# One tile of the selective scan filled by TensorE and ScalarE instead of through DRAM

## The reference

```
x = x + 0.5 * ffn(layernorm(x))      # fp4 quantised, 256 -> 704 -> 256
x = x + mixer(layernorm(x))          # selective scan, below
x = x + 0.5 * ffn(layernorm(x))
```

```
xz = h @ in_proj_w;  u, z = split(xz);  u = silu(causal_conv(u))
dt, B, C = split(u @ x_proj_w);  delta = softplus(dt @ dt_proj_w + b)
h_t[d, n] = exp(delta_t[d] * A[d, n]) * h_{t-1}[d, n] + delta_t[d] * u_t[d] * B_t[n]
y_t[d] = sum_n h_t[d, n] * C_t[n] + u_t[d] * D[d]
out = (y * silu(z)) @ out_proj_w
```

## Time and profile before

| | us |
|---|---|
| device time, median of 3 runs | 3021.85 (3017.2 to 3024.54) |
| device time of the profiled execution | 3027.0 |
| its span, first to last instruction | 3025.2 |
| PE busy | 2607.9 (86%) |
| DVE busy | 2569.9 (85%) |
| POOL busy | 2276.9 (75%) |
| ACT busy | 1756.1 (58%) |
| mean granted TensorE clock | 0.90 of full speed |

### The profile page before, as it was taken

The page is one execution under the profiler, slowest core; times in us unless marked ns, Lnnn a source line. Parts: engine busy times, 40 slices in busy tenths (PEclk is TensorE's granted clock), DMA queues, the critical chain, the costliest instruction groups (busy, mean ns, idle before and its releaser), DMA issues. The chain is left out here.

```text
span 3025.2 us, 31486 instructions
## 1 busy us (share of the span) xinstructions
PE 2607.9 (86%) x10147; PEld 1368.9 (45%) x10147; DVE 2569.9 (85%) x2435; ACT 1756.1 (58%) x2337; POOL 2276.9 (75%) x1348
## 2 busy tenths in 40 slices
PE   4999999967878878878878879879877669999998
PEld 2666657633424424424425425425422126666665
DVE  7888875539999999999999999999999967777775
ACT  3554444447766766766767766767765434444442
POOL 4766664249989989989989899899899855655652
PEclk9999999978979979979979979979967679999999
DMA  3111111038898898888988988988988940011000
GB/s 112 32 53 42 53 49 35 24 101 213 196 220 204 204 220 198 209 213 200 213 215 200 218 212 198 214 207 208 217 197 203 233 97 28 29 35 35 28 29 21
DMA packets 183588, 424.67 MB, mean 140 GB/s; under 512 B 23952, under 2 KB 91472, under 8 KB 183184
## 3 DMA queue, kind: packets, MB, share of 16 engines
q1 hardware_dynamic: 164544, 402.19, 54.1%
q10 hardware_dynamic: 18896, 20.65, 2.4%
HBM read 341.88 MB, written 55.71 MB: 131 GB/s over the span
## 5 line engine op out<-in xcount | busy, mean ns | idle before, releaser
L1475 POOL TENSOR_TENSOR mix_scan<-mix_scan,mix_bc 128x1024 f32<-128x1024 f32 x512 | 1199.3, 2358 | 180.3 <-DVE mix_scan L1572 180.0
L1572 DVE TENSOR_TENSOR_SCAN mix_scan<-mix_decay,ps_all 128x1024 f32<-128x1024 f32 x512 | 1166.5, 2284 | 71.4 <-ACT ps_all L1516 24.4
L885 PE MATMUL ps_all<-ffn_w_gate_up,ffn_xT 128*128 128x512 f32 (+1 forms) x1536 | 654.0, 562 | 13.7 <-DVE ffn_h L612 9.4
L1525 ACT ACTIVATE mix_decay<-mix_decay,mix_a_neg 128x1024 f32<-128x1024 f32 x512 | 575.0, 1142 | 105.1 <-DMA mix_decay<-delta_rows 103.6
L1626 PE MATMUL ps_all<-mix_stack,mix_sel 96*128 96x512 bf16 x896 | 317.6, 442 | 322.5 <-DVE mix_scan L1572 309.2
L1582 DVE TENSOR_TENSOR ps_all<-ps_all,mix_bc 128x1024 f32<-128x1024 f32 x448 | 541.0, 1208 | 20.6 <-PE ps_all L1626 20.5
L885 PEld LDWEIGHTS ps_all<-ffn_w_gate_up,ffn_xT 128*128 128x128 f32 x1536 | 278.6, 192 | 245.9 <-issue 201.1
L758 POOL TENSOR_TENSOR ffn_h_scaled<-ffn_h,ffn_h_recip 128x1408 f32<-128x1408 f32 x64 | 168.6, 2635 | 243.6 <-ACT ffn_h_recip L853 243.6
L1608 PE MATMUL ps_all<-mix_scan,mix_red 128*32 128x512 f32 x2048 | 336.2, 738 | 7.7 <-POOL mix_scan L1475 7.7
L612 DVE TENSOR_TENSOR ffn_h<-ffn_silu_gate,ps_all 128x704 f32<-128x704 f32 x128 | 113.6, 887 | 269.6 <-ACT ffn_silu_gate L800 266.0
L1626 PEld LDWEIGHTS ps_all<-mix_stack,mix_sel 96*128 96x128 bf16 x896 | 69.1, 102 | 599.4 <-DVE mix_scan L1572 409.9
(11 more groups left out here) (132 smaller groups left out, 3835.5 us busy)
## 6 DMA issues: line engine op xcount, KB each, us to landing
mix_decay<-delta_rows SPq DMA_DIRECT2D x512, 512.0 KB, 9.6
mix_dbu_aside<-delta_u_rows SPq DMA_DIRECT2D x64, 512.0 KB, 10.7
mix_stack<-mix_parts SPq DMA_DIRECT2D x384, 64.0 KB, 2.5
delta_rows<-mix_delta SPq DMA_DIRECT2D x32, 512.0 KB, 3.1
ffn_x<-_attn_hidden_states_dram SPq DMA_DIRECT2D x32, 256.0 KB, 2.9
after_ffn<-ffn_y SPq DMA_DIRECT2D x32, 256.0 KB, 3.0
normed_ffn<-ffn_y_normed SPq DMA_DIRECT2D x32, 256.0 KB, 3.1
mix_x_tokens<-normed_ffn SPq DMA_DIRECT2D x32, 256.0 KB, 12.8
```

What stands on the lines that cost most here:

```text
L885: ins = M(psG[:, lo:hi], xT[:, j % 2, (t * KX + k) * P:(t * KX + k + 1) * P], wgu[:, k, lo:hi], start=(k == 0), stop=(k == KX - 1))
L1475: G.tensor_tensor(wt, wt, bc[r % 2][:, 1, :], ALU.mult).then_inc(hc_done, 1)
L1525: A.activation(da[:, at % SPREADS, :], da[:, at % SPREADS, :], ACT.Exp, scale=const.aneg[:, qi:qi + 1]).then_inc(exp_done, 1)
L1572: V.tensor_tensor_scan(w[:, slot % RING, :], da[:, slot % SPREADS, :], ps_du[:, slot % 2, :], 0.0, ALU.mult, ALU.add).then_inc(scan_done, 1)
```

## The change

GpSimd's tile `aside` is no longer read from DRAM. A new kind of job, R, is added to the table: 16 a round, two for each tile aside. A job R is one matmul with the same operands as one half of `replicate` (96 rows, 512 columns, bf16) into the job's bank, and ScalarE copies it from there into half of `aside` (L1317 of the changed kernel). The jobs stand at the slots 8k and 8k+1 for the tile of slot 8k+7 (57 and 58 for the last), behind the other jobs of the same slot. GpSimd waits for the second copy instead of the transfer. `keep_du`, `spread_du`, the DRAM tensor `delta_u_rows` and their semaphores are gone.

```
-PER_BATCH = {"T": 4, "P": 8, "C": 16, "X": 4, "B": 4, "D": 8, "Z": 8, "O": 4}
+JOBS = sorted(JOBS + [(8 * k + h + (k == 7), "R", 2 * k + h) for k in range(8) for h in range(2)], key=lambda job: job[0])
+PER_BATCH = {"R": 16, "T": 4, "P": 8, "C": 16, "X": 4, "B": 4, "D": 8, "Z": 8, "O": 4}
...
-        rel = {"O": -1, "Z": 0}.get(kind, 1)
+        rel = {"O": -1, "Z": 0, "R": 0}.get(kind, 1)
...
-    du_dram = nc.dram_tensor("delta_u_rows", [2, CHUNKS, P - ASIDE_FROM, L], F32, kind="Internal").ap()
...
-    def keep_du(sy, b, par, c):
-        sy.wait_ge(du_done, chunk(b, c))
-        sy.dma_start(du_dram[par, c, :, :], du[ASIDE_FROM:P, :]).then_inc(du_kept, 16)
...
     def leave1(pool, n):
         pool.wait_ge(cast1, n)
-        pool.wait_ge(du_kept, 16 * n)
...
+        elif kind == "R":
+            c, s = divmod(EVERY * (n // 2) + EVERY - 1, SLOTS)
+            i, q = divmod(s, 4)
+            h = n % 2
+            ins = nc.tensor.matmul(job, const.sel[0:SEL, i, :], stack[:, c % 2, q, h * 512:(h + 1) * 512],
+                                   start=True, stop=True)
...
+        elif kind == "R":
+            k, h = divmod(n, 2)
+            if not (b == 0 and k == 0):
+                act.wait_ge(aside_put, b * (64 // EVERY) + k)
+            nc.scalar.activation(aside[:, h * 512:(h + 1) * 512], job, ACT.Copy).then_inc(taken[kind], 1)
...
-            def spread_du(r, R, slot):
-                c, s = divmod(slot, SLOTS)
-                if s == EVERY - 1:
-                    sy.wait_ge(du_kept, 16 * chunk(R, c))
-                if slot >= EVERY or r > 0:
-                    sy.wait_ge(aside_put, nth_aside(R, slot) - 1)
-                row = 32 * (s % 4) + 8 * (s // 4) - ASIDE_FROM
-                sy.dma_start(aside[:, :],
-                             du_dram[r % 2, c, row:row + NCH, :].unsqueeze(0).to_broadcast([NST, NCH, L]))\
-                  .then_inc(aside_in, 16)
...
                     if core(rr, full) and is_aside(at):
-                        pool.wait_ge(aside_in, 16 * nth_aside(R2, at))
+                        pool.wait_ge(taken["R"], 2 * nth_aside(R2, at))
```

More of the change, by code:

```diff
@@ L1002 @@
 EVERY, ASIDE_IN, ASIDE = 8, 7, 4
-ASIDE_FROM = 104
 def round_jobs(r, n_batches, full):
@@ L1071, in mixer @@
     delta_dram = nc.dram_tensor("delta_rows", [2, DI, L], F32, kind="Internal").ap()
-    du_dram = nc.dram_tensor("delta_u_rows", [2, CHUNKS, P - ASIDE_FROM, L], F32, kind="Internal").ap()
     S = a.sem
-    du_kept, aside_in, aside_done, aside_put = S("du_kept"), S("aside_in"), S("aside_dbu_done"), S("aside_put")
+    aside_done, aside_put = S("aside_dbu_done"), S("aside_put")
     x_in = [S("x_in0"), S("x_in1")]
-    made = {k: S("made_" + k) for k in "TPCXBDZO"}
-    taken = {k: S("taken_" + k) for k in "TPCXBDZO"}
+    made = {k: S("made_" + k) for k in "TPCXBDZOR"}
+    taken = {k: S("taken_" + k) for k in "TPCXBDZOR"}
     hist = S("conv_history")
@@ L1331, in first_sync @@
             keep_delta(sy, 0, 0, 0)
-            keep_du(sy, 0, 0, 0)
         if k in (43, 44):
@@ L1448, in program @@
                             keep_delta(sy, b, rb % 2, cc)
-                        if s - LATER[c] == CAST1:
-                            keep_du(sy, b, rb % 2, cc)
                         for part, when in enumerate((CAST1, CAST2, CAST3)):
@@ L1453, in program @@
                                 restack(sy, b, cc, part)
-                    rr, R2, at = ahead(r, R, slot, ASIDE_IN)
-                    if core(rr, full) and is_aside(at):
-                        spread_du(rr, R2, at)
                     rr, R2, at = ahead(r, R, slot, SPREAD)
```

## The result

| | before | after |
|---|---|---|
| device time, median | 3021.47 us (4 runs) | 3160.78 us (4 runs, 3159.62 to 3163.59) |
| ratio, with its 95% interval | | 1.0458 (1.0445 to 1.047) |
| span of the profiled execution | 3025.2 us | 3158.0 us |
| mixer, first to last scan of VectorE | 1785.9 us | 1921.7 us |

The forecast was 3131 us in 3075 to 3190. The direction and the places were right; the size was 30 us short: 109 us in place of 139. By the profiled executions the increase is 3159.76 - 3027.0 = 132.8 us, since the profiled execution of before lay 5 us above its median.

The account below looks back on a forecast made before the run. The prediction took VectorE, 95% busy in the mixer, as the bound. Its terms, 65 + 39 + 8 - 3 = 109 us on the median-adjusted 3021.85, gave 3131 us, range 3075 to 3190.

Parts of the forecast that it names:

- Bound and slack: Mixer: VectorE, 95% busy, sets the pace; TensorE's 309 us of waiting for scans is slack that counts slot by slot.
- Place A: Slots 0 to 4: Z1 must wait until ScalarE has taken Z0, delaying slot 4; 65 us, bounds 52 and 82.
- Place B: Slots 25 to 29: Z3 must wait until Z2 is taken, starting 4.2 us later; 39 us, bounds 28 and 52.
- Place C: Slot 8 on: C0 waits until O0 is taken, making slot 11's replicate 0.7 us late in six rounds; 4 us.
- Removed transfers: Mixer: lower DMA load shortens VectorE's waits for exponentials; -3 us, bounds 0 and -8.
- Occupancy at nothing: Mixer: 38 to 64 us of TensorE matmuls and 77 us of ScalarE copies fit in idle time, costing nothing.
- Place D: Slot 17 on: two jobs R around O1 cost TensorE 0.7 us directly in six rounds; 4 us.
- The clock one: Rival: after the stalls TensorE's clock stays low through later jobs; +170 us, 3192 us; chance 20%.
- The covered stalls: Rival: Z0 is taken before TensorE wants Z1, leaving only occupancy; about +20, 3042 us; chance 8%.
- the transfer as brake: Rival: fewer transfers let ScalarE run earlier, so the kernel gets faster; -8 to -32, 2990 to 3014 us; chance 3%.
- the fourth: Rival: the new kernel does not wait as written, so Z1 does not wait for Z0; no change; chance 3%.

Follow-up runs that it names:

- e8: Kernel before, with all aside transfers but the first shrunk to 8 of 128 partitions: 3016.77 us beside 3020.85, ratio 0.9989.
- e9: Changed kernel, R pairs for the tiles of slots 7, 15, 31, 55 together in slots 0, 7, 24, 48: 3027.59 us, ratio 1.0006 to before.
- e1: Changed kernel, both jobs R for a round's first aside tile put in slot 0 ahead of its other jobs: 3085.2 us, ratio 1.0202 to before.
- e7: Changed kernel, with 24 and 10 extra matmuls nobody needs ahead of Z1 and Z3 to keep TensorE busy: 3133.99 us, ratio 1.0371 to before.
- e2: Changed kernel, both jobs R for the tile of slot 31 put in slot 24 ahead of its other jobs: 3113.53 us, ratio 1.0297 to before.
- e3: Changed kernel, both jobs R for the tile of slot 15 put in slot 8 ahead of the output projection: 3140.29 us, ratio 1.0384 to before.
- e5: Changed kernel, R pairs for the tiles of slots 7, 15, 31 together in slots 0, 8, 24, ahead of other jobs: 3034.2 us, ratio 1.0043.
- e6: Changed kernel, R pairs for the tiles of slots 7, 15, 31, 55 together in slots 0, 8, 24, 48, ahead of other jobs: 3033.42 us, ratio 1.0048.

## Why the prediction was right, and where it fell short

**Bound and slack: right.** VectorE's busy time in the mixer did not change (1717.5 us against 1714.5), and TensorE's 309 us of waits did not cover the delays at places A, B and C.

**Removed transfers: right, as far as e8 tells.** -3 us forecast, -3.3 measured there with the transfers shrunk. The mixer's DMA share fell from 0.86 to 0.71, more than the tenth that was forecast, since the same stretch is also 7% longer. VectorE's own waits after the change, as those in the earlier trace rows:

```profile
DVE mix_scan L1559 <- ACT ps_all L1503: 28.4, 29, 2.5
...
DVE mix_scan L1559 <- ACT mix_decay L1512: 5.2, 3, 2.6
```

For the decay it waits 5.2 us in place of 8.1, for the aside tile's copy 28.4 in place of 24.4: slot 15 has 8.0 us more (place C), slot 47 3.3 less. The decay tiles land after 7.6 us (9.6 before), which took only these 2.9 us from VectorE's waits for the decay.

**Occupancy at nothing: right within some 5 us.** e9 has all of it, for a ratio of 1.0006, but without the transfers. e8, with them shrunk and nothing added, is at 0.9989. The difference, 0.17% or 5 us, is an estimate of what the new work costs in e9, with bounds of about 1 and 9 us from the two intervals. Its profile has 8.8 us more than before in slots 2 to 4, where the first pair stands.

**Place A: right, in steps and size.** Z1 was to start 1356.9 - 1340.21 = 16.7 us after slot 0's scan; in the fourth round after the change it starts at 1404.13, 16.69 us after that scan (1387.44). TensorE idled 5.50 us (5.5 forecast). The gate came 9.1 us late in this round: 6.5 of waiting, 1.9 of Z1 at the low clock, and the rest from the `replicate` behind it at 1.06 us and `sum_quad`, which I had granted the high clock. That is 69.5 for 65 us; e1 shows the cause, e7 splits it.

**Place B: right, sized 8 us low.** Z3 was to start 4.2 us later; against the scan of slot 26 it did in the fourth round (4.56 us behind it, 0.38 before). Of the difference, 4 us are the last round, which I set at 1 us because no sequence follows: it cost 5.3, since VectorE still wants its `replicate` on time in slots 28 and 29. The rest is again the low clock reaching past Z3 (the `replicate` behind it took 1.00 us). e2 shows the cause.

**Place C: the mechanism right, the term mis-sized.** The step that failed is "`replicate` of slot 11 moves to 1377.9, and VectorE ... gets it at 1378.5: 0.7 us". It let C0 run at 1.89 us after its pause; it took 2.8 to 3.6. I had named 3 us each as the upper bound if the clock is low there, and took a value near the lower end. Measured: 16.2 us where the term had 4. It also left out what the late C0 pushes on, through TensorE's jobs up to slot 13, to ScalarE's copy of the aside tile for slot 15: 8.0 us. Together 20 of the 30 us that the sum was short. e1 and e3 show both.

**Place D: wrong, small.** +4 forecast, -2.6 measured. The new jobs do not make this gain: slots 19, 47 and 54 are 2.6, 3.3 and 2.5 us shorter after the change, and 2.4, 3.1 and 3.2 us shorter in e8, which has no job R. So it comes with the lighter transfers or from the one profiled execution of before; which of the two stays open. Slot 49, where I had put nothing, has +6.1 us. It is 0.4 in e9, which pairs its R, but -0.3 in e7, which does not, so its cause stays open too.

**The rivals.** The clock one was right on the places and wrong in extent: Z1 and Z3 ran low in 15 of 16 cases, but two or three jobs later the clock was high again, and its price of 170 us lies 31 above the measured 139. The Trainium skill's rule (TensorE: Matmul & The Clock Gate, section A second HAM failure mode: psum-queue depth-cycling) fits with these stretches of 0.50. In this case the loss shows only where a pause falls ahead of work that VectorE waits for, and the mean clock, 0.85 against 0.84 before, does not show it at all. The covered stalls are refuted by the 16 waits, the transfer as brake by the result and by e8, and the fourth by the wait of Z1 for the silu.

## What to carry to other kernels

Where jobs alternate between two PSUM banks, one job put in between gives every later job another neighbour to wait for: list which result each job now waits for and where its consumer stands. Place new jobs so that the jobs VectorE depends on keep their old neighbours, and not as a pair right ahead of a long job; e9 did it with four pairs, one of them in an empty slot, and four windows left split. A wait of TensorE of some microseconds ahead of work that the bounding engine needs is to be priced at both clock levels, and so is a shorter one: 2.72 us ahead of C0 were followed by the low clock in the changed kernel and not in e1. Gains measured one at a time add up only if no two of them hold the same microseconds.

## What was unexpected of the hardware

- Matmuls that compute nothing anyone needs made the changed kernel 27 us faster. By the profile 19.5 us of this stand at slot 4, where they began without a gap and kept the clock up (Z1 1.98 in place of 3.78 us). Begun after 1.90 us of waiting they did not keep it up: the clock fell 0.4 us later, they took 0.40 us each for 0.22, and held up the work they were meant to help.
- The length of a pause alone does not tell the clock behind it: after the same 2.72 us one C0 took 3.58 us (changed kernel, fourth round) and the other 2.00 (e1).
- With a ninth of the large DMA transfers shrunk, the rest landed after 9.0 us in place of 9.6, and this was worth 3.3 us of 3021. In the changed kernel, without them and 5% slower, they landed after 7.6 us.
- The better placements scatter more than the kernel before beside them: 15.8 us over 12 runs in e9, against 8.9 over the 17 runs of before in the same comparison. The profiles of e5 and e6 have one and two rounds with an extra at slot 10, that of e9 none; what makes the scatter was not tested.
